# A CIN tower with its group order, product ring, low-part lag and gather position changed

## The reference

```python
for idx, (W, b) in enumerate(params):            # W: 39 x fk x 128, fk = 39, 64, 64
    z = jnp.einsum('bhd,bkd,hks->bsd', x0, xk, W) + b[None, :, None]
    z = jax.nn.relu(z)
    # layers 0 and 1: first 64 channels become the next xk, the other 64 go out
    # layer 2: all 128 go out
logit = jnp.sum(jnp.concatenate(direct, axis=1), axis=-1)      # over d
h = relu(concat([logit, dense_ctx]) @ W_top1 + b_top1)
h = relu(h @ W_top2 + b_top2);  y = h @ W_top3
```

## Time and profile before

| | us |
|---|---|
| median of 3 runs | 636.41 (634.5 to 636.77) |
| the profiled execution's own time | 634.96 |
| its span | 633.2 |
| PE busy | 605.3 (96%) |
| DVE busy | 552.1 (87%) |
| POOL busy | 462.8 (73%) |
| ACT busy | 304.0 (48%) |

### The profile page before, as it was taken

The page is one execution under the profiler, slowest core; times in us unless marked ns, Lnnn a source line. Parts: engine busy times, 40 slices in busy tenths (PEclk is TensorE's granted clock), DMA queues, the critical chain, the costliest instruction groups (busy, mean ns, idle before and its releaser), DMA issues.

```text
span 633.2 us, 7282 instructions
## 1 busy us (share of the span) xinstructions
PE 605.3 (96%) x1938; PEld 365.6 (58%) x1938; DVE 552.1 (87%) x513; ACT 304.0 (48%) x375; POOL 462.8 (73%) x294
## 2 busy tenths in 40 slices
PE   0887999999999999999999999999999999999998
PEld 0334665656666665656666665656666665656663
DVE  1675999999999999999999999999999999999660
ACT  2142646545354545545364545555364545554323
POOL 6848587878878787878878787878788787718250
PEclk9999899999999999999999999999999999999998
DMA  7699797878869494968869494958769494942000
GB/s 254 164 231 218 151 214 146 191 164 183 183 147 216 96 220 92 223 126 186 166 148 216 103 219 91 224 119 198 155 161 206 107 219 98 221 89 79 2 0 0
DMA packets 29184, 98.59 MB, mean 156 GB/s; under 512 B 8210, under 2 KB 17170, under 8 KB 21235
## 3 DMA queue, kind: packets, MB, share of 16 engines
q1 hardware_dynamic: 22312, 93.81, 66.6%
q0 software_dynamic: 5120, 1.32, 1.7%
q10 hardware_dynamic: 1738, 3.33, 1.4%
HBM read 94.60 MB, written 3.84 MB: 155 GB/s over the span
## 4 chain that ended last, share of the span: by engine, by line
PE 89%; DMA 5%; SPq 2%; POOL 2%; issue 1%; ACT 1%; DVE 1%; ACTq 0%
PE z L634 42%; PE z L640 13%; PE z L642 12%; PE z L645 12%; DMA x_rep<-x_rows 4%; PE z L624 4%; PE z L628 2%; PE z L627 2%; POOL gathered L418 1%; PE d_products L721 1%; SPq L319 1%; SPq L311 1%; PE z L695 1%; DMA gathered<-in_tables,rows_sb 0%; DMA x_rows<-gathered 0%
## 5 line engine op out<-in xcount | busy, mean ns | idle before, releaser
L357 POOL TENSOR_TENSOR low<-products,high 128x1024 fp32r<-128x1024 f32 x128 | 303.8, 2389 | 104.2 <-ACT high L762 93.8
L475 DVE TENSOR_TENSOR products<-x_rep,xk 128x1024 f32<-128x1024 f32 (+1 forms) x258 | 333.1, 1338 | 21.1 <-ACT xk L746 13.3
L634 PE MATMUL z<-products,w_whole 128*128 128x512 f32 x640 | 296.5, 593 | 0.1
L762 ACT ACTIVATE high<-products 128x1024 fp32r<-128x1024 f32 x128 | 135.2, 1056 | 133.1 <-DVE products L475 124.7
L418 POOL DMA_INDIRECT gathered<-in_tables,rows_sb x160 | 157.5, 984 | 44.4 <-issue 41.8
L640 PE MATMUL z<-high,w_high 128*128 128x512 f32 x352 | 183.8, 522 | 3.1 <-ACT high L762 3.1
L634 PEld LDWEIGHTS z<-products,w_whole 128*128 128x128 f32 x640 | 121.5, 190 | 104.0 <-issue 92.8
L642 PE MATMUL z<-high,w_low 128*128 128x512 f32 x352 | 138.9, 395 | 0.0
L645 PE MATMUL z<-low,w_high 128*128 128x512 f32 x352 | 109.9, 394 | 1.6 <-POOL low L357 1.4
L640 PEld LDWEIGHTS z<-high,w_high 128*128 128x128 f32 x352 | 66.3, 188 | 41.4 <-issue 24.9
L642 PEld LDWEIGHTS z<-high,w_low 128*128 128x128 f32 x352 | 66.5, 189 | 37.0 <-issue 26.5
(11 more groups left out here) (54 smaller groups left out, 179.8 us busy)
## 6 DMA issues: line engine op xcount, KB each, us to landing
x_rep<-x_rows SPq DMA_DIRECT2D x60, 768.0 KB, 14.7
x_rep<-x_rows SPq DMA_DIRECT2D x60, 512.0 KB, 5.8
x_rep<-x_rows SPq DMA_DIRECT2D x19, 256.0 KB, 4.2
x_rows<-gathered SPq DMA_DIRECT2D x16, 225.0 KB
x_rep<-in_w ACTq DMA_DIRECT2D x2, 1280.0 KB, 9.5
gathered<-in_tables,rows_sb POOLq DMA_INDIRECT x160
x_same<-x_rows SPq DMA_DIRECT2D x15, 78.0 KB
x_same<-x_rows SPq DMA_DIRECT2D x16, 64.0 KB
```

Of the source, the lines that this page charges most:

```text
L357: ops.tensor_tensor(low[0:p, slot, 0:n, :], product(index, p, n), high[0:p, slot, 0:n, :].bitcast(fp32), ALU.subtract).then_inc(low_by[kin ...
L475: nc.vector.tensor_tensor(slots, rep, row.unsqueeze(1).broadcast_to([p, n, N]), ALU.mult).then_inc(made, 1 + pair)
L634: mm = nc.tensor.matmul(out, w_whole[0:p, at, i, :], product(index, p, n)[:, i, :], start=(first and i == 0), stop=(last and i == n - 1))
L762: nc.scalar.activation(high[0:p, slot, 0:n, :], product(index, p, n), ACT.Copy).then_inc(rounded, 1)
```

## The change

- `KINDS`: layer 1 goes from wpwpwppwdh to ppwpdpwpdh, layer 0 from wsdw to wdws, layer 2 from wwpwpdpwph to wwwwpwppwh.
- `RING` goes from 8 to 7, `SEL_SLOT` from 0 to 6, and `SELECTED` is reordered so that the stacked tile of layer 0 comes last.
- `LOW_LAG` goes from 1 to 2: DVE makes a low part two groups after its product.
- `GATHERS`: the ten gathers are issued after index 15, where one was issued after index 1 and nine after index 6.
- `logits2` comes after index 9 and not 8, `logits01` one index earlier, `after_layer2` ahead of index 4 and not 3, `after_layer1` ahead of index N1 + 5 and not N1 + 3.

```diff
--- before.py
+++ after.py
@@ -59,7 +59,7 @@
 
 PARTS = [(0, 4), (4, 8), (8, 14), (14, T1)]
 FIRST_PARTS = [(4, 6), (0, 2), (2, 4), *((t, t + 2) for t in range(6, T1, 2))]
-SELECTED = [0, 1, 6, 2, 3]
+SELECTED = [0, 1, 2, 3, 6]
 assert all(row_of(1, end - 1) - row_of(1, first) == end - 1 - first for first, end in PARTS + FIRST_PARTS)
 
 
@@ -87,7 +87,7 @@
 STACKED = "whole, its second tile split and stacked"
 ALONE = "one tile of 64 partitions, split and stacked"
 LETTER = {"w": WHOLE, "d": LOW_DVE, "p": LOW_POOL, "h": STACKED, "s": ALONE}
-KINDS = {1: "wpwpwppwdh", 0: "wsdw", 2: "wwpwpdpwph"}
+KINDS = {1: "ppwpdpwpdh", 0: "wdws", 2: "wwwwpwppwh"}
 
 
 def groups_of(layer, tiles, partitions):
@@ -117,7 +117,7 @@
 ENDS = {1: N1 - 1, 0: N1 + N0 - 1, 2: len(BODY) - 1}
 
 RINGED = [i for i, g in enumerate(BODY) if g[4] != LOW_DVE]
-RING = 8
+RING = 7
 PART_RING = 3
 TURN = -(-len(RINGED) // RING) * RING
 PART_TURN = -(-len(SPLIT) // PART_RING) * PART_RING
@@ -126,10 +126,10 @@
 PAIRED = [0,2]
 assert all(RINGED.index(i) % 2 == 0 and RINGED.index(i + 1) == RINGED.index(i) + 1 for i in PAIRED)
 assert all(BODY[i][:1] == BODY[i + 1][:1] and BODY[i][3] == BODY[i + 1][3] for i in PAIRED)
-GATHERS = {1: 1, 6: 9}
+GATHERS = {15: 10}
 assert sum(GATHERS.values()) == GB
-LOW_LAG = 1
-SEL_SLOT = 0
+LOW_LAG = 2
+SEL_SLOT = 6
 assert all(RINGED.index(i) % RING != SEL_SLOT for i in LAYER0 if i in RINGED)
 WARM = min(WHOLES.index(i) for i in LAYER0 if i in WHOLES)
 LATE = (LOW_DVE, STACKED, ALONE)
@@ -567,9 +567,9 @@
                         late.append((c, index))
                     while late and late[0][1] <= index - LOW_LAG:
                         make_low(*late.pop(0))
-                    if index == 8 and not (isinstance(c, int) and c == 0):
+                    if index == 9 and not (isinstance(c, int) and c == 0):
                         logits2(c - 1)
-                    if index == N1 + N0 + 3:
+                    if index == N1 + N0 + 2:
                         logits01(c)
                 if isinstance(c, int) and c in (-1, C - 1):
                     while late:
@@ -796,13 +796,13 @@
                 for index in range(len(BODY)):
                     if index == (N1 if first else 2) and not last:
                         copy_same(c + 1)
-                    if index == 3 and not first:
+                    if index == 4 and not first:
                         after_layer2(c - 1, first=isinstance(c, int) and c == 1)
                     if last and index == N1:
                         act.wait_ge(dense_loaded, 16 * 6)
                         act.wait_ge(used, count("all", c, DENSE_FROM))
                         nc.scalar.activation(dense_parts, dense_rows, ACT.Copy).then_inc(dense_rounded, 1)
-                    if index == N1 + 3:
+                    if index == N1 + 5:
                         after_layer1(c)
                     if index == N1 + N0 + 3 and not last:
                         after_layer0(c)
```

## The result

| | before | changed |
|---|---|---|
| median of 16 runs each, us | 636.62 | 633.14 |
| ratio, 95% interval | | 0.9953 (0.9941 to 0.9965) |
| profiled execution, us | 634.96 | 630.71 |
| its span | 633.2 | 628.9 |

The forecast was 634.0 in 631.3 to 638.6 and "within 0.5%" the likeliest; measured are 3.5 us between the medians, 0.47% by the ratio. In two repetitions of the changed kernel the ratio was 0.9948 (0.9929 to 0.9967) and 0.9964 (0.9943 to 0.9985). The profiled execution of the changed kernel was the fastest of its 16, so its 4.25 us less overstates the gain.

The account below looks back on a forecast made before the run. It took PE's bare work, 35.48 us per chunk, as the bound. Start -2.4 and steady state 0.0 gave 632.6 from the profiled 634.96, or 634.0 from the median 1.45 above that; range 631.3 to 638.6.

Parts of the forecast that it names:

- Steady state bound by PE, no gain from the order: In every chunk: PE's bare work takes 35.48 us with unchanged group counts, so reordering without a hole gains 0.0.
- Due times: Layers 1 and 2 of each chunk: every part worked out against PE's start of layer 1, each ready when due.
- The one called tight: Low part of index 1 at layer 1's head: POOL done at 1.6, PE wants it at 2.3, margin 0.7 us.
- rival 2: Slower: index 1's low part late in every chunk once its chain slips over 0.7 us; 5.4 us, 639.4; chance 0.12.
- The stack of index 23: On DVE between POOL's low parts of 21 and 0: a full port hit costs 1.8 us, priced as nothing on path.
- Ring: DVE's product ring: with 7 places 21 members make three full turns, every product waits for the seventh before; no cost.
- after_layer1: Between layers 1 and 2: ACT reaches this after the high part of s, about 14.4, no later than before.
- The start: Chunk 0: layer 2 begins on PE at 64.7, layer 1 of chunk 1 at 80.9 against 83.31, 2.4 us sooner.
- the new wait: Layer 1 of chunk 0: PE reaches index 8's low part at 54.9, ready at 56.6, a wait of 1.7 us.
- Sum: Whole kernel: -2.4 us from the start and 0.0 from steady state, tail unchanged.
- Rival 1: Chunk 0: PE's new waits there fall away and `xk[1]` is the bound; gain -3.6 us, 632.8; chance 0.15.
- Rival 3: Chunk 1 or 2: the start's gain is lost again because loads come no sooner; 636.4 us; chance 0.13.

Follow-up runs that it names:

- e6_gather_between: The changed kernel with one of ten gathers moved from behind index 15 to between POOL's low parts of index 0 and 1; 642.52 us, one run.
- e4_ring8: The changed kernel with eight places in the product ring, not seven; 644.65 us, ratio 1.0145 to the kernel before.
- e7_l0_alone: The kernel before with only layer 0's new word wdws and the new order of selected tiles; 651.43 us, ratio 1.0247 to the kernel before.
- e9_l0_and_layer1: The kernel before with layer 0's word wdws, the new order of selected tiles and `after_layer1` at N1 + 5; 634.00 us, ratio 0.9973.
- e1_after: The changed kernel run again, nothing altered, as reference for its set; 632.09 us, ratio 0.9948 to the kernel before.
- e12_after_again: The changed kernel run once more, nothing altered, in the last set; 633.44 us, ratio 0.9964 to the kernel before.
- e3_lag1_first: The changed kernel with DVE's low parts one group later, not two, in chunk 0 alone; 634.24 us, ratio 0.9973 to the kernel before.
- e10: The changed kernel with the second `x0_rep` part cut to tiles 4 to 6, the third one tile longer; 633.78 us, ratio 0.9968 to before.
- e2_old_l0: The changed kernel with layer 0's old word wsdw and the old order of selected tiles; 634.93 us, ratio 0.9985 to the kernel before.
- e8_warm_tail: The changed kernel with one extra float32 matmul while PE waits in the tail for the last logits; 632.12 us, ratio 0.9940 to before.

## Why the prediction was right

- *Steady state bound by PE, no gain from the order.* Right: 35.44 for 35.48, no PE wait in it. The 0.04, 0.5 us in all, was not in the sum, and the prediction had called any other period than 35.48 a sign of being wrong. Both halves of the words have a share: 35.46 with the old words of layers 1 and 2, 35.45 with the old word of layer 0. Its cause is open.
- *Due times.* All held. The one called tight was: 0.45 us for 0.7. The point of rival 2 was thus nearer than stated, and e6_gather_between is rival 2 made real: 0.88 us per chunk. That it did not happen in the changed kernel was right with 0.12 against it. The stack of index 23, feared for the shared port, is not clear of POOL's low part of 21: at 288.63 it starts 0.43 us before that ends, and takes 0.97 us where 0.69 is usual. It is off the path, as said.
- *Ring.* "No cost" is right for 7 places, but the working beside it followed only the wait at index 4 and gave the eight places no cost in the new order; e4_ring8 shows 0.84 us per chunk.
- *after_layer1.* The sum had "no later", right; that with the new word the old place can cost 36.71 - 35.46 = 1.25 us per chunk (e7_l0_alone against e9_l0_and_layer1) it did not see. Both have the old words of layers 1 and 2; in the changed kernel itself the old place was not run.
- *The start.* The step by step holds to some hundredths in e1_after (5.74 behind part 1), and the new wait was 1.85 for 1.7. The term that was left out is the clock: the profiled execution began layer 2 at 6.42 behind part 1 and not at 5.74, 0.7 us lost behind the wait. In return POOL was not late in layer 2, and 2.15 us came out for 2.4.
- *Sum.* -2.4 for medians 3.5 apart, ratios between 0.9948 and 0.9964. Start and 0.5 of the chunks make 2.7, from one trace of the kernel before; the remainder of 0.8 has no term in the sum. The record shows where such a remainder can come from: the two kernels don't run equally often at the full clock.

| mean granted clock of an execution | before, set of e1 | e1_after | before, set of e12 | e12_after_again |
|---|---|---|---|---|
| 0.997, mean us (executions) | 634.1 (6) | 631.6 (4) | 633.8 (15) | 632.2 (5) |
| 0.995 | 635.7 (5) | 632.9 (3) | 635.2 (5) | 633.6 (3) |
| 0.992 | 636.9 (18) | 634.0 (3) | 636.8 (14) | 634.7 (3) |

At the same granted clock the changed kernel is 1.6 to 2.9 us faster, which is what the sum gives. But the kernel before was at 0.992 in 32 of these 63 executions and the changed kernel at 0.992 or less in 7 of 24. The sum has no term for that; whether it comes of the holes that the change closes is not shown. The call of "within 0.5%" held narrowly: by the ratio it is 0.47%, while the medians are 3.48 / 636.62 = 0.55% apart. With a sum that is 1 us short, being on this side of the border is in part luck.

Rival 1 (more of the start) fell: e3_lag1_first removed the early wait and won nothing, and 5.74 to 5.76 us behind part 1 was the best start of layer 2 seen with the new words. Rival 3 (gain lost to the loads of chunk 2) fell as well, DVE has no wait for `x0_rep` behind 59 us.

Not tested by themselves are the lag of 2 in the loop, the new places of `logits2`, `logits01` and `after_layer2`, and each new word of layers 1 and 2. e9_l0_and_layer1 has all of these old, and its ratio can't be told from the changed kernel's.

## What to carry to other kernels

Where PE has no idle time in the loop, an equal count of group kinds in another order gained 0.1% there (0.04 us of 35.48) and the rest in the start; look for the arrival that sets the start and put what needs it last. Such an order is a package: one word alone was 2.5% slower than the kernel before, the package with one other ring size 1.4%, with the old gather places 26%. The due times foresaw the last and missed the first two, which the waits in the traces then named. Count a ring by the distance in members at each position and not by its places: here 21 members in 7 places are seven back everywhere, in 8 places only five at the head of the turn.

## What the runs showed of the hardware

- The spread between runs, 630.7 to 635.7 us for the same code, goes with the granted clock (table above) and arises in the start and the tail. e12_after_again, 3.1 us longer in span than the first profiled execution, is 1.47 us behind it at 102 us, still 1.47 at 563, and loses 1.7 more in the 16 matmuls of the tail (8.82 for 7.13).
- Part 1 of the same load arrived between 58.95 and 61.34 us. In three of the fourteen profiled executions (e10 to e12) DVE stood still for 2.4 to 4.2 us at a time between two products of the start, with nothing in the profile that it can have waited for then. What holds it was not tried.
- The lower clock behind a hole of the start was not a fixed price. After PE's wait of 1.85 us near 56 us the granted clock of the stretch from 54 to 66 was 0.86 in one execution; after waits of 1.76 (e1_after), 2.01 (e2_old_l0), 2.96 (e8_warm_tail) and 3.34 us (e4_ring8) in the same place it was 1.00.
